# Gate, LoRA-A and output columns in three split products each, dealt out as a 408-column and a 256-column piece

## The reference

```python
# layer 1, adapter chosen per batch
y   = x @ W + (x @ A[idx[b]]) @ B[idx[b]]            # rank 16
# layer 2, regrouped to 4 x 256 rows; 8 experts of rank 16
z   = y @ W_base.T + b_base
lg  = y @ W_gate.T                                   # 8 logits
p   = top-2 softmax of lg, renormalised over the two
h   = y @ A_e.T                                      # 8 experts x 16 = 128 columns
out = x + z + (h * p[expert]) @ B_e
```

## Time and profile before

| | |
|---|---|
| median of 3 runs | 69.65 us (69.59 to 70.81) |
| the profiled execution | 69.46 us |
| its span, from the first to the last instruction | 67.8 us |
| PE busy | 63.6 us, 94% |
| DVE, ACT, POOL busy | 49%, 39%, 15% |
| granted TensorE clock, mean of its records | 1.0 |

### The profile page before, as it was taken

The page is one execution under the profiler, slowest core; times in us unless marked ns, Lnnn a source line. Parts: engine busy times, 40 slices in busy tenths (PEclk is TensorE's granted clock), DMA queues, the critical chain, the costliest instruction groups (busy, mean ns, idle before and its releaser), DMA issues.

```text
span 67.8 us, 1120 instructions
## 1 busy us (share of the span) xinstructions
PE 63.6 (94%) x340; PEld 54.2 (80%) x340; DVE 33.2 (49%) x126; ACT 26.2 (39%) x69; POOL 10.3 (15%) x30
## 2 busy tenths in 40 slices
PE   3999999999999999999999999999999999999920
PEld 3988898888888898888988988988988988988700
DVE  0034887000991799368517638428428428128100
ACT  4272873004972566123045324324324321321430
POOL 1000998703093001010010010010010000000000
PEclk9999999999999999999999999999999999999999
DMA  0899999996000056552004040040040040040044
GB/s 0 251 292 347 393 372 409 406 403 230 4 21 4 12 135 141 121 130 49 0 5 155 0 155 10 0 155 0 0 155 5 0 155 0 0 155 0 10 154 156
DMA packets 4648, 8.45 MB, mean 125 GB/s; under 512 B 793, under 2 KB 1049, under 8 KB 4642
## 3 DMA queue, kind: packets, MB, share of 16 engines
q1 hardware_dynamic: 4178, 7.70, 33.7%
q0 software_dynamic: 320, 0.54, 2.1%
q10 hardware_dynamic: 144, 0.13, 0.6%
HBM read 5.26 MB, written 2.10 MB: 109 GB/s over the span
## 4 chain that ended last, share of the span: by engine, by line
PE 94%; ACT 1%; issue 0%; DVE 0%
PE bank L426 17%; PE bank L428 16%; PE bank L427 16%; PE bank L450 12%; PE bank L434 7%; PE bank L512 5%; PE bank L505 4%; PE bank L518 4%; PE bank L515 4%; PE bank L486 3%; PE bank L526 2%; PE bank L472 1%; PE bank L493 1%; ACT y_out L290 1%; PE bank L482 1%
## 5 line engine op out<-in xcount | busy, mean ns | idle before, releaser
L426 PE MATMUL bank<-c_hi,x_hi 128*128 128x512 f32 x32 | 14.2, 443 | 0.0
L428 PE MATMUL bank<-c_hi,x_lo 128*128 128x512 f32 x32 | 12.6, 393 | 0.0
L427 PE MATMUL bank<-c_lo,x_hi 128*128 128x512 f32 x32 | 12.6, 392 | 0.0
L450 PEld LDWEIGHTS bank<-c_gh,x_raw 128*128 128x128 f32 x64 | 9.1, 189 | 0.7
L450 PE MATMUL bank<-c_gh,x_raw 128*128 128x152 f32 x64 | 9.6, 292 | 0.0
L428 PEld LDWEIGHTS bank<-c_hi,x_lo 128*128 128x128 f32 x32 | 6.0, 188 | 1.3
L290 ACT COPY y_out<-bank 128x512 f32<-128x512 f32 (+1 forms) x9 | 4.8, 541 | 5.4 <-PE bank L428 5.4
L426 PEld LDWEIGHTS bank<-c_hi,x_hi 128*128 128x128 f32 x32 | 6.0, 189 | 0.8
L241 POOL COPY c_gh<-lora_raw 128x64 f32<-128x64 f32 x8 | 2.5, 317 | 27.0 <-PE bank L450 27.0
L296 ACT CAST xa_t<-bank 128x128 fp32r<-128x128 f32 x8 | 2.1, 266 | 11.6 <-PE bank L472 11.5
L427 PEld LDWEIGHTS bank<-c_lo,x_hi 128*128 128x128 f32 x32 | 6.1, 190 | 0.5
(11 more groups left out here) (79 smaller groups left out, 105.0 us busy)
## 6 DMA issues: line engine op xcount, KB each, us to landing
x_raw<-x_t SPq DMA_DIRECT2D x8, 256.0 KB, 7.3
out<-y_out SPq DMA_DIRECT2D x7, 256.0 KB, 2.0
w_raw<-fold_in SPq DMA_DIRECT2D x4, 324.0 KB, 4.8
w_raw<-fold_in SPq DMA_DIRECT2D x4, 256.0 KB, 5.0
bw_rows<-bw_hi SPq DMA_DIRECT2D x8, 81.0 KB, 2.1
lora_raw<-lora POOLq DMA_DIRECT2D x8, 64.0 KB, 5.1
bw_rows<-bw_lo SPq DMA_DIRECT2D x4, 81.0 KB, 2.1
ffn_b_raw<-ffn_b SPq DMA_DIRECT2D x1, 256.0 KB, 8.3
```

The costliest lines, as they stand in the source:

```text
L426: nc.tensor.matmul(out, a_hi, b_hi, start=first, stop=False)
L427: nc.tensor.matmul(out, a_hi, b_lo, start=False, stop=False)
L428: return nc.tensor.matmul(out, a_lo, b_hi, start=False, stop=last)
L450: mm = nc.tensor.matmul(g_bank[n][:, own_cols(t)], x_raw[:, t, c, :], c_gh[:, c, own_cols(t)], start=(c == 0), stop=(c == KC - 1), skip_gr ...
```

## The change

The three groups of columns that every product shares are now one array of 648 columns: 8 gate, 128 expert and 512 output columns, `wg_hi` and `wg_lo`. Every product with it is dealt out in two pieces in separate PSUM banks: a left one with the gate, the experts and the first 256 output columns (392 columns; 408 with the 16 LoRA-A columns), and a right one with the last 256 output columns. All of it is split float32r, three matmuls for each piece. What is left in f32 is the first chunk's gate and expert columns in the fold.

In the fold, `bw` comes last, behind the last chunk of C. C is `cl_hi`/`cl_lo` (left) and `cr_hi`/`cr_lo` (right). In the tiles `Left(t)` takes the place of `G(t)` and half of `Z(t)`, `Right(t)` that of the other half; `Lora(t)` has two matmuls and `Delta(t)` six. There are three banks for left pieces and two for right ones. `T1` transposes 98 rows instead of 128. POOL now makes a `hi` and a `lo` of the LoRA-A columns. The output copy of a tile is two copies of 256 columns; for the last tile the right one is DVE's.

```diff
-        wb_hi = sb("wb_hi", [P, KC, D], F32R)
-        wb_lo = sb("wb_lo", [P, KC, D], F32R)
+        wg_hi = sb("wg_hi", [P, KC, WIDE], F32R)
+        wg_lo = sb("wg_lo", [P, KC, WIDE], F32R)
...
+            def fold_pass(m, w, wg):
+                cols = slice(GH, LEFT) if m == 0 else slice(0, LEFT)
+                for i in range(KC):
+                    rows = slice(i * P, (i + 1) * P)
+                    nc.tensor.matmul(bank[i][:, cols], w[:, m, rows], wg[:, m, cols], ...)
+                    nc.tensor.matmul(fold_right(i), w[:, m, rows], wg[:, m, LEFT:], ...)
...
+            def Left(t, chunks):
...
+                    mm = product(left(t)[:, own_cols(t)], x_hi[:, t, c, :], x_lo[:, t, c, :],
+                                 cl_hi[:, c, own_cols(t)], cl_lo[:, c, own_cols(t)], c == 0, False)
+            def Right(t, chunks):
...
+                    product(right(t), x_hi[:, t, c, :], x_lo[:, t, c, :], cr_hi[:, c, :], cr_lo[:, c, :], False, False)
+            def Lora(t):
...
+                nc.tensor.matmul(left(t)[:, LORA_LEFT], xa_t[0:ROWS, t % 2, :], bw_rows[:, t // 2, 0:LEFT], ...)
+                nc.tensor.matmul(right(t), xa_t[0:ROWS, t % 2, :], bw_rows[:, t // 2, LEFT:], ...)
+            def Delta(t):
...
+                pe.wait_ge(hw_lo_done, t + 1)
+                product(left(t)[:, OUT_LEFT], ..., ffn_b_hi[:, 0:HALF], ffn_b_lo[:, 0:HALF], ...)
+                product(right(t), ..., ffn_b_hi[:, HALF:], ffn_b_lo[:, HALF:], ...)
...
+            for m in range(KC):
+                b_hi, b_lo = ...
+                product(bwl_bank[:, 0:LEFT], b_hi, b_lo, wg_hi[:, m, 0:LEFT], wg_lo[:, m, 0:LEFT], m == 0, m == KC - 1)
+                mm = product(bwr_bank[:, 0:HALF], b_hi, b_lo, wg_hi[:, m, LEFT:], wg_lo[:, m, LEFT:], m == 0, m == KC - 1)
+            mm.then_inc(bw_summed, 1)
+
+            Left(0, (0, 1, 2, 3))
+            Left(1, (0,))
             T1(0)
+            Left(1, (1, 2, 3))
+            Lora(0)
+            Right(0, (0, 1))
             T1(1)
+            Right(0, (2, 3))
+            Lora(1)
             T2(0)
+            Left(2, (0, 1))
+            Delta(0)
+            Left(2, (2, 3))
+            T2(1)
             for t in range(2, NT):
+                Right(t - 1, (0, 1))
+                T1(t)
+                Right(t - 1, (2, 3))
+                Lora(t)
+                Delta(t - 1)
                 if t + 1 < NT:
+                    Left(t + 1, (0, 1, 2, 3))
+                    T2(t)
+            Right(NT - 1, (0, 1, 2))
             T2(NT - 1)
+            Right(NT - 1, (3,))
+            Delta(NT - 1)
```

More of the change, by code:

```diff
@@ L44 @@
 GH = E + ER
-WIDE = D + GH
+WIDE = GH + D
+HALF = D // 2
+LEFT = GH + HALF
+OWN = R + LEFT
 TOP = 2
@@ L84, in adaln_ffn_kernel @@
         bias_lo = sb("bias_lo", [1, D], F32R)
-        c_hi = sb("c_hi", [P, KC, D], F32R)
-        c_lo = sb("c_lo", [P, KC, D], F32R)
-        c_gh = sb("c_gh", [P, KC, R + GH + R])
+        cl_hi = sb("cl_hi", [P, KC, OWN + R], F32R)
+        cl_lo = sb("cl_lo", [P, KC, OWN + R], F32R)
+        cr_hi = sb("cr_hi", [P, KC, HALF], F32R)
+        cr_lo = sb("cr_lo", [P, KC, HALF], F32R)
         bw_hi = sb("bw_hi", [P, WIDE], F32R)
@@ L113, in adaln_ffn_kernel @@
         bank = [ctx.enter_context(nc.psum_tensor(f"bank{i}", [P, 512], F32)) for i in range(8)]
[L114 to L118, removed]
+        left_bank = bank[0:3]
+        right_bank = bank[4:6]
+        t1_bank, t2_bank = bank[3], bank[6]
+        bwl_bank, bwr_bank = bank[6], bank[7]
         wa_loaded = [sem(f"wa_loaded{m}") for m in range(KC)]
@@ L342, in _, with split_left, split_right @@
                 split_x(t)
-            dve.wait_ge(bw_hi_done, 1)
[L344 to L357, removed]
+            def split_left(i):
+                dve.wait_ge(cl_hi_done, i + 1)
+                lo(cl_lo[:, i, LORA_LEFT], bank[i][:, 0:LEFT], cl_hi[:, i, LORA_LEFT], cl_lo_done)
+            def split_right(n):
+                dve.wait_ge(cr_hi_done, n + 1)
+                lo(cr_lo[:, 2 * n:2 * n + 2, :].rearrange("p c n -> p (c n)"), bank[4 + n][:],
+                   cr_hi[:, 2 * n:2 * n + 2, :].rearrange("p c n -> p (c n)"), cr_lo_done)
+            dve.wait_ge(ident_ready, 1)
+            for i in range(2):
+                dve.wait_ge(cl_summed, i + 1)
+                diag = bank[i][:, GH + i * P:GH + (i + 1) * P]
+                nc.vector.tensor_tensor(diag, diag, ident[:], ALU.add).then_inc(cl_plus_i, 1)
+            for i in range(KC):
+                split_left(i)
+            dve.wait_ge(cr_summed, 2)
+            for n in range(2):
+                diag = bank[5][:, n * (HALF + P):n * (HALF + P) + P]
+                add = nc.vector.tensor_tensor(diag, diag, ident[:], ALU.add)
+            add.then_inc(cr_plus_i, 1)
+            for n in range(2):
+                split_right(n)
+            dve.wait_ge(ffn_b_hi_done, 1)
+            lo(ffn_b_lo[:], ffn_b_raw[:], ffn_b_hi[:], ffn_b_lo_done)
+            dve.wait_ge(bw_hi_done, 1)
+            lo(bw_lo[:, 0:LEFT], bwl_bank[:, 0:LEFT], bw_hi[:, 0:LEFT], bw_lo_done)
+            dve.wait_ge(bw_hi_done, 2)
+            lo(bw_lo[:, LEFT:], bwr_bank[:, 0:HALF], bw_hi[:, LEFT:], bw_lo_done)
             steps = [0]
@@ L424, in product @@
             def product(out, a_hi, a_lo, b_hi, b_lo, first, last):
-                nc.tensor.matmul(out, a_hi, b_hi, start=first, stop=False)
-                nc.tensor.matmul(out, a_hi, b_lo, start=False, stop=False)
-                return nc.tensor.matmul(out, a_lo, b_hi, start=False, stop=last)
-            def fold_gh(m):
-                pe.wait_ge(wa_loaded[m], DMA)
-                for i in range(KC):
-                    mm = nc.tensor.matmul(cgh_bank[i], w_raw[:, m, i * P:(i + 1) * P], raw_gh(m),
-                                          start=(m == 0 and i in (0, 3)), stop=(m == KC - 1), skip_group_check=True)
-                return mm
@@ L454, in Z @@
-            def Z(t, chunks):
-                pe.wait_ge(x_lo_done, t + 1)
-                for c in chunks:
-                    pe.wait_ge(c_lo_done, c + 1 if t == 0 else KC)
-                    if c == 0 and t < 4:
-                        pe.wait_ge(c_lo_done, t + 1)
-                    if c == 0 and t >= 4:
-                        pe.wait_ge(y_done, t - 3)
-                    product(c_bank[t % 4][:], x_hi[:, t, c, :], x_lo[:, t, c, :], c_hi[:, c, :], c_lo[:, c, :], c == 0, False)
+                nc.tensor.matmul(out, a_hi, b_hi, start=first, stop=False, skip_group_check=True)
@@ new lines, in product @@
+                nc.tensor.matmul(out, a_hi, b_lo, start=False, stop=False, skip_group_check=True)
+                return nc.tensor.matmul(out, a_lo, b_hi, start=False, stop=last, skip_group_check=True)
+            def fold_pass(m, w, wg):
+                cols = slice(GH, LEFT) if m == 0 else slice(0, LEFT)
+                for i in range(KC):
+                    rows = slice(i * P, (i + 1) * P)
+                    nc.tensor.matmul(bank[i][:, cols], w[:, m, rows], wg[:, m, cols],
+                                     start=False, stop=False, skip_group_check=True)
+                    nc.tensor.matmul(fold_right(i), w[:, m, rows], wg[:, m, LEFT:],
+                                     start=(m == 0 and w is wt_hi and wg is wg_hi and i % 2 == 0), stop=False, skip_group_check=True)
@@ L503, in _ @@
             pe.wait_ge(zeros_ready, 1)
             for _ in range(WARM_UPS):
-                nc.tensor.matmul(bwgh_bank[:, 0:P], zeros[:].bitcast(mybir.dt.bfloat16), zeros[:].bitcast(mybir.dt.bfloat16),
+                nc.tensor.matmul(bwr_bank[:, 0:P], zeros[:].bitcast(mybir.dt.bfloat16), zeros[:].bitcast(mybir.dt.bfloat16),
                                  start=True, stop=True)
+            pe.wait_ge(wa_loaded[0], DMA)
+            for i in range(KC):
+                nc.tensor.matmul(bank[i][:, 0:GH], w_raw[:, 0, i * P:(i + 1) * P], raw_gh(0),
+                                 start=True, stop=False, skip_group_check=True)
@@ L507, in _ @@
             for m in range(KC - 1):
-                fold_gh(m)
                 pe.wait_ge(w_hi_done, 2 * m + 2)
-                for i in range(KC):
-                    nc.tensor.matmul(c_bank[i][:], wt_hi[:, m, i * P:(i + 1) * P], wb_hi[:, m, :], start=(m == 0), stop=False)
+                fold_pass(m, wt_hi, wg_hi)
                 pe.wait_ge(w_lo_done, 2 * m + 1)
-                for i in range(KC):
-                    nc.tensor.matmul(c_bank[i][:], wt_lo[:, m, i * P:(i + 1) * P], wb_hi[:, m, :], start=False, stop=False)
+                fold_pass(m, wt_lo, wg_hi)
@@ L516, in _ @@
                 pe.wait_ge(w_lo_done, 2 * m + 2)
-                for i in range(KC):
-                    nc.tensor.matmul(c_bank[i][:], wt_hi[:, m, i * P:(i + 1) * P], wb_lo[:, m, :], start=False, stop=False)
-            fold_gh(KC - 1).then_inc(cgh_summed, 1)
-            pe.wait_ge(lora_loaded, NT * DMA)
+                fold_pass(m, wt_hi, wg_lo)
```

(15 more changed lines are left out.)

287 lines of the change are left out of this document (142 added, 145 removed).

## The result

The changed kernel takes 71.57 us (71.22 to 71.92) against 69.62: ratio 1.030, with a 95% interval of 1.025 to 1.034. It is slower; the prediction was 69.1, with a range that ended at 70.8. The profiled execution took 71.81 us, its span 70.1.

A forecast was written before the change was run, and what follows sets the result against it. PE (TensorE) bounds the kernel, busy 63.6 of 67.8 us. Of 2.9 us saved on PE, 2.9 go into waits and 0.4 returns from the shorter last copy: span 67.4, time 69.1, range 67.3 to 70.8.

The forecast's parts named there:

- PE's work: TensorE's work in fold and tiles, priced part by part: without waits PE would save 2.9 us.
- steady tile: One tile's PE work in the middle of the kernel: 4.81 us instead of 5.06, with no wait.
- narrow matmul: Split matmul of 256 columns in fold and tiles: interpolated at 0.117 us, between ends of 0.109 and 0.130.
- Rival C: Slower: weight loads do not hide behind 256 columns, 0.130 for each of 152 narrow matmuls, +2.0, thus 71.1; chance 0.11.
- Wait at T1(0): Entry to the tiles: PE waits 0.9 us for DVE's xa_rows, from 25.95 to 26.8.
- nothing ahead of it moves: Entry to the tiles: DVE's four x_lo, behind the LoRA load, stay at 18.06 to 20.5 as before.
- Lora(0): Tile 0: PE waits 0.3 us for the first spread of bw_lo to land, at 28.87.
- Delta(0): First Delta: PE waits 0.9 us for hw_lo, which comes late because DVE does gate(1) first; start at 33.05.
- T1(2): Tile 2's T1: PE waits 0.2 us for xa_rows, from 35.66 to 35.9.
- Of 2.9 us saved on PE, 2.9 go into waits: Whole-kernel account: waits take the full PE saving, and 0.4 comes back from the shorter last copy.
- seven microseconds: Kernel before: the same spreads began at 22.4, seven microseconds ahead of Lg(0).
- The last hw_lo: End of the kernel: PE waits 0.6 us for tile 7's hw_lo before the last Delta.

The follow-up runs named there:

- e1: The changed kernel run again with no edit: 71.09 us, ratio 1.024 to the kernel before.
- e3: The changed kernel with DVE splitting xa_rows of tile 0 ahead of ffn_b_lo and bw_lo: 71.1 us, ratio 1.021 to the kernel before.
- e9: The kernel of e6 run again, unedited, as partner of e10: 71.05 us, ratio 1.022 to the kernel before.
- e10: The kernel of e6 plus 22 matmuls of zeros in PE's list ahead of T1(0): 69.92 us, ratio 1.006 to the kernel before.
- e6: The changed kernel with hw of tile 0 split ahead of gate(1) on DVE and exp_top(1) on ACT: 71.2 us, ratio 1.023 to the kernel before.
- e7: The changed kernel with early bias and x splits, earlier hw of tile 0, and Lora(7) ahead of Right(6)'s last chunk: 67.73 us, ratio 0.977.
- e11: The kernel before, with chunks 1 to 3 of each tile's output columns as two 256-column products instead of one of 512: 70.02 us, ratio 1.006.
- e4: The changed kernel with DVE's x_lo of tiles 2 and 3 moved behind xa_rows of tile 0: 69.89 us, ratio 1.006 to the kernel before.

## Why the prediction was wrong, point by point

**PE's work: right.** Forecast for a steady tile 4.81, measured 4.89. The narrow matmul in a tile is 0.120 (forecast 0.117), the 408-column one 0.186 (0.183), as the distances in the timeline after show:

```profile
46.67 0.35 PE L452 MATMUL bank<-cl_lo,x_hi 128*128 128x408 f32 x1
46.86 0.35 PE L453 MATMUL bank<-cl_hi,x_lo 128*128 128x408 f32 x1
...
47.39 0.28 PE L453 MATMUL bank<-cr_hi,x_lo 128*128 128x256 f32 x1
47.51 0.28 PE L451 MATMUL bank<-cr_hi,x_hi 128*128 128x256 f32 x1
```

I interpolated both from overheads that end at the fold's pace, 0.228 for 512 columns; the tiles of the kernel before already ran at 0.231. That is 0.4 us from Lora(2) to Lora(7). The rule N/2.4 + 2.5 ns (the Trainium skill, TensorE: Matmul & The Clock Gate, Back-to-back issue gap), given there for an isolated warm matmul, would be 0.109 and 0.173; this trace disagrees with both. Rival C's 0.130 did not come either.

**The waits: each at its place, the first mis-sized, and this is the step that failed.** "Wait at T1(0): 0.9 us" was 1.9 to 2.1. Three things went in. In the first trace PE came 0.6 earlier (in e1's it did not: 25.9). I had built on the trace of before, whose first split matmuls start 0.43 us apart for 512 columns, which is the pace of 1.2 GHz, though the clock row of that profile has a 9 there. Its chain of waits has 1.50 for the first four of them and 0.91 for the next four:

```profile
5.99 1.50 PE bank L512 x4
7.49 0.91 PE bank L515 x4
```

In the first trace after, narrow ones are 0.12 apart from 5.50 on, so that stretch is shorter. The row of ACT and DVE work took 10.83 from `lb_hi` to T1(0), where my sum was 10.6. And its origin, the start of `lb_hi`, lay at 16.64 here and at 16.5 to 17.35 in the other traces of this arithmetic (18.24 in e3's). The prediction says of `x_lo` that it "stands behind the load of the LoRA matrices" and that "nothing ahead of it moves": it took the landing from one trace of before, where `lb_hi` starts at 16.20, and gave it no spread, while it worked out every link behind it.

**What a wait does besides waiting: not in the forecast at all.** I priced idle time of PE at its length. e9 and e10 show that behind the hole at T1(0) the clock also falls to half, in some executions, for about 1 us. Of the 2.7 us by which the first trace missed, 0.7 stand at T1(0) and 1.1 are the half clock. Without it the kernel still takes 71.09 (e1), so this is the smaller part: of the 2.1 between forecast span and e1's (69.5), 0.95 is the later landing (17.15; 0.5 of this because the copies were issued later in that execution), 0.25 the longer row, 0.1 comes at Lora(0) (30.16), 0.15 by Delta(0) (34.5), 0.1 by T1(2) (37.46) and 0.5 by Lora(7) (62.80), in the steady tiles.

**The other waits.** Lora(0): 0.3 forecast, 0.35 where the clock stayed up (e1: 0.53 between the starts, 0.19 of it columns). Delta(0): 0.9 forecast, 0.9 measured, and the edit of e6 gives it back. T1(2): 0.2 and 0.2. The prediction's "seven microseconds" between the first spreads and `Lg(0)` in the kernel before are 6.5 (22.42, 28.97); nothing hangs on it. The last hw_lo: 0.6 forecast; the starts are 0.61 apart, 0.12 of it columns, so 0.5.

**The signs.** "Of 2.9 us saved on PE, 2.9 go into waits" had the right account with the wrong sum on the second side. The rival that ended slower was put on the matmul (C); the slower end came from the other side of the account. The prediction has no rival in which the waits are longer than forecast.

## What to carry to other kernels

When a rearrangement frees the bound engine, follow the row of work that must now be done sooner back to the event that it hangs on, and ask how far that event moves from run to run. In front of such an event, do whatever does not need it: here five operations on each of ACT and DVE, moved ahead of one wait, turned a loss of 2.4% into a gain of 1.3%. A hole in PE's list is to be priced with what it does to TensorE's clock, and filling it with matmuls of zeros is a cheap test of that. An edit that makes a result ready sooner gains only if what uses it moves as well (Lora(7) and T2(7) in e7).

## What the runs showed that was not expected

- The slowest of the eight LoRA copies landed 5.6 to 6.1 us after its issue in nine traces of the changed arithmetic and 5.2 in e3's, whose copies were issued 2 us later than the others'; it is 5.2 to 5.3 in the three of the kernel before and its variants. The requests are the same. The landing is 0.5 us or so later by this, which is in every loss above; why was not tried.
- The landing can stop PE in the arithmetic of before too. In e11's trace the split matmuls of 512 columns are 0.23 apart from 5.5 on, earlier than in that of the kernel before (7.1). PE is through with its `fold_gh` at 16.3 and then waits for `lb_lo`:

```profile
17.82 0.35 PE L531 MATMUL bank<-w_raw,lb_raw 128*128 128x136 f32 x1 [1.36 <-DVE lb_lo L325]
```

- A half clock of 3.4 us behind 2 us without matmuls, in 2 of 4 executions of the changed kernel, 0 of 4 of its repeat and 7 of 8 of e6's kernel, which differs from it only behind the hole. Why it is more frequent there stays open. Behind e4's shorter hole (1.7 us between the end of the columns and T1(0)) it was in 0 of 10.
